# Output projection, norm and next products in one block by halves of the tokens

## The chip, the cores and the metric

The kernel runs on one core of a Trainium2 chip. The metric is the device time of one execution in microseconds, the median of several runs. TensorE does the matrix products into PSUM, VectorE (DVE) and ScalarE (ACT) work on SBUF and PSUM, GpSimd (POOL) on SBUF, and SyncE (SP) issues nearly all the DMAs.

## What is computed

The reference is two layers of a perceiver over 16 sequences of 64 tokens of 256 features, all float32. The part that matters here, cut:

```python
x = x + cross_attention(layernorm(x), ctx)         # 16 heads, 1601 keys
x = x + wide_attention(layernorm(x), context)      # 8 heads of 128, 1024 keys, Wout 1024 -> 256
x = x + merged_ffn(layernorm(x))                   # gates from relu(xn @ gate_w1 + b1), mean over tokens
x = x + shared_attention(layernorm(x), ctx)        # 16 heads of queries, one head of 1601 keys
x = x + alibi_attention(layernorm(x))              # 16 heads of 16, 64 keys, Wo 256 -> 256
h = layernorm(x)                                   # last layer: attention with rotary q and k,
x = x + moe(h)                                     # on rmsnorm(h) * ln1, then 8 experts, top 2
```

## The kernel before

`x` stays in SBUF as eight tiles of 128 tokens by 256 features (`TILES`), and is held by token. A product needs its input by feature, so each norm ends with 16 transposes on TensorE into four PSUM banks, which ScalarE moves into `xn_t` by halves of 512 tokens (`HALVES`). Everything is written in blocks: a block holds one instruction stream for each engine, ordered by hand with semaphores, and ends in a barrier of all engines.

Between an attention and the next products there are two blocks.

`add_projection` (a `dense_block`) does the output projection. TensorE fills one unit for each tile of tokens: 2 chunks of features for shared and alibi attention, 8 for the wide one, and a float32 product is two matmul instructions in the trace. VectorE adds the unit to `x` (L342), takes the statistics (L345) and aggregates them into `moments` (L346). Four units of two banks go round.

`norm_block` does the rest. SP issues the loads of this block and of what follows. VectorE adds epsilon to all eight variances at once (L163), ScalarE takes the root (L222), VectorE refines and inverts it in five small steps (L150 to L154), each waiting for the one before, and writes the eight normalized tiles (L177). The MoE norm does this twice, the second time into `again` (L170 to L187). TensorE transposes tile by tile (L200), ScalarE moves each half (L227), and then the tasks run in two units of two banks: TensorE multiplies (L215) and VectorE or ScalarE moves the result out (L320, L321, L326, L1923, L2180 to L2182). The tasks are

- FFN: two tasks of `gate_w1`, each over both halves, moved by VectorE and by ScalarE in turn;
- alibi: two tasks each of `wk` and `wq`, then four value tasks; GpSimd multiplies the attention's bias (L2143) when the loads are in;
- MoE: four rotary tasks of `wk`, four of `wq` (each with the swapped weights as well), all moved by VectorE in three operations, then four value tasks moved by ScalarE.

After the key tasks SP issues the copies of the keys into `k_blocks`, eight DMAs, and the block waits for them before it ends.

The norm ahead of shared attention has no tasks. It fills rows 64 and up of the three key and three query buffers with zeros, six memsets of GpSimd (L133). In `shared_attention_block` GpSimd then sets row 64 of the key buffers to one, the ones and zeros of `v`, the zeros of `k_blocks`, and adds the output bias to `x`. TensorE makes the four query units, SP stores and reloads them, and the ring of scores for the maxima (L1718, VectorE's L1812) starts when the first are back.

Of the kernel before, what the change touches and what calls it, by code (L numbers as in the profile page):

```python
# [12 lines left out]
F32 = mybir.dt.float32  # L13
I32 = mybir.dt.int32
ALU = mybir.AluOpType
# [3 lines left out]
P = 128  # L19
# [4 lines left out]
BANK = 512  # L24
# [213 lines left out]

def dense_block(core, name, tasks, copies=(), pool_program=None):
# [60 lines left out]


def feature_products(weights, m, src_t, chunks=CHUNKS, rows=P, cols=P):

    return [(lambda u, h=h: u[0:cols, h, :], weights[:, k, m * cols:(m + 1) * cols],
             src_t[:, k, h * BANK:(h + 1) * BANK], k == 0, k == chunks - 1, h)
            for h in range(HALVES) for k in range(chunks)]


def feature_tasks(core, jobs):

    nc = core.nc
    tasks = []
    for weights, m_tiles, src_t, dst, bias, relu in jobs:
        for m in range(m_tiles):
            def move_dve(unit, step, m=m, dst=dst, bias=bias, relu=relu):
                out = dst[:, m, :].rearrange("p (h n) -> p h n", h=HALVES)
                if bias is None:
                    return nc.vector.tensor_copy(out, unit)
                if relu:
                    return nc.vector.tensor_scalar(out, unit, bias[:, m:m + 1], 0.0, ALU.add, ALU.max)  # L320
                return nc.vector.tensor_scalar(out, unit, bias[:, m:m + 1], None, ALU.add)  # L321

            def move_act(unit, step, m=m, dst=dst, bias=bias, relu=relu):
                out = dst[:, m, :].rearrange("p (h n) -> p h n", h=HALVES)
                func = ACT.Relu if relu else (ACT.Copy if bias is None else ACT.Identity)
                return nc.scalar.activation(out, unit, func, bias=0.0 if bias is None else bias[:, m:m + 1])  # L326

            on = ("dve", "act")[len(tasks) % 2]
            tasks.append((feature_products(weights, m, src_t), move_dve if on == "dve" else move_act, on))
    return tasks  # L330
# [688 lines left out]
def wide_attention(core):  # L1019
# [5 lines left out]
    with ExitStack() as outer:  # L1025
# [14 lines left out]
        add_projection(core, "wide_out", heads_t, WIDE_HEADS, wout, x)  # L1040
# [232 lines left out]
def merged_ffn(core):  # L1273

    nc, dram, x = core.nc, core.dram, core.x
    with ExitStack() as outer:
        def sb(stack, name, shape):
            return core.sbuf(stack, f"ffn_{name}", shape)  # L1280

        xn_t, gate_t = (sb(outer, n, [P, CHUNKS, TOKENS]) for n in ("xn_t", "gate_t"))
        gate_tiles = {n: sb(outer, n, shape) for n, shape in (
            ("gw2", [P, CHUNKS, TASKS]), ("gw2_wide", [P, CHUNKS, P]), ("gb2_column", [TASKS, 1]), ("gb2_wide", [P, 1]),
            ("spread_mask", [P, SPREAD]), ("task_b1", [GATE_ROWS, HIDDEN]), ("task_b2", [GATE_ROWS, DIM]))}
        with ExitStack() as inner:
            gw1, gb1 = sb(inner, "gw1", [P, CHUNKS, DIM]), sb(inner, "gb1", [P, CHUNKS])
            xn = sb(inner, "xn", [P, TILES, DIM])
            norm_block(core, "ffn_norm", x, xn, xn_t, True, loads=[(gw1[:], dram["gate_w1"]), (gb1[:], dram["gate_b1"])] + [
                (t[:], dram[n]) for t, n in ((gate_tiles["gw2"], "gate_w2"), (gate_tiles["gw2_wide"], "gate_w2_wide"),  # L1290
                                             (gate_tiles["gb2_wide"], "gate_b2_wide"), (gate_tiles["spread_mask"], "spread_mask"),
                                             (gate_tiles["task_b1"], "ffn_task_b1"), (gate_tiles["task_b2"], "ffn_task_b2"))]
                + [(gate_tiles["gb2_column"][:], dram["gate_b2"].unsqueeze(1))],
                tasks=feature_tasks(core, [(gw1, CHUNKS, xn_t, gate_t, gb1, True)]), task_loads=2, moments_ready=True)
        merged_ffn_block(core, xn_t, gate_t, gate_tiles)


def merged_ffn_block(core, xn_t, gate_t, gate_tiles):

# [233 lines left out]
def shared_attention(core):  # L1533
# [3 lines left out]
    with ExitStack() as outer:  # L1537
        def sb(stack, name, shape, dtype=F32):
            return core.sbuf(stack, f"shared_{name}", shape, dtype)

        wo, heads_t = sb(outer, "wo", [P, CHUNKS, DIM]), sb(outer, "heads_t", [P, CHUNKS, TOKENS])
# [7 lines left out]
                   fills=[(t[SPLIT_ROWS:].bitcast(F32), 0.0) for t in (*k, *q)],  # L1549
# [4 lines left out]
        add_projection(core, "shared_out", heads_t, CHUNKS, wo, x)  # L1554


def shared_attention_block(core, k, q, wq, bq, v, v1, bv, bo, scratch, heads_t):
# [17 lines left out]
    with ExitStack() as stack:  # L1575
# [28 lines left out]
        queries_stored = sem("queries_stored")  # L1604
        ones_set = sem("ones_set")
# [30 lines left out]
        with core.block() as block:  # L1636
# [275 lines left out]
def value_tasks(nc, xn_t, wv, v):  # L1912
# [4 lines left out]
    for b0 in range(0, BATCH, per_unit):  # L1917
# [8 lines left out]
        tasks.append((products, move, "act"))  # L1926
    return tasks


# [919 lines left out]
```

## Time and profile before

| what | value |
|---|---|
| runs | 2371.7, 2373.8, 2376.3 us; median 2373.8 |
| profiled execution | 2377.7 us, span 2375.9 us |
| TensorE busy | 2179.1 us, 92% of the span |
| mean granted clock of TensorE | 0.952 |

The profile is one execution. A timeline row is a run of like instructions: its start in the span, its length from first start to last end, engine, line of the kernel, operation, result and operands, count, and in brackets how long the engine was idle before it and what it waited for. L50 in a bracket is the barrier between two blocks.

### The profile page before, as it was taken

How to read it: one execution, taken by the hardware profiler on the slowest of the kernel's cores; microseconds unless marked ns; L12 is line 12 of the kernel's file. 1: busy time of each engine (PE TensorE's matmuls, PEld its weight loads, DVE VectorE, ACT ScalarE, POOL GpSimd, SP SyncE). 2: the span in 40 equal slices, each digit the busy share in tenths (PEclk: the TensorE clock that was granted, in tenths of full speed). 3: DMA queues.
4: the chain of work that ended last, by engine and by line, in shares of the span. 5: the costliest groups of instructions: out<-in, count | busy, mean ns of one | idle time of the engine just before them, and what ended most of it. 6: DMA issues, size and time to landing. Idle time of an engine off the chain costs nothing. (4 is left out here: it accounts for less than half of the span.)

```text
span 2375.9 us, 39783 instructions
## 1 busy us (share of the span) xinstructions
PE 2179.1 (92%) x15922; PEld 1507.1 (63%) x15922; DVE 1314.4 (55%) x2266; ACT 994.0 (42%) x1858; POOL 332.1 (14%) x366
## 2 busy tenths in 40 slices
PE   7999999999999977999998799978999998877796
PEld 4777777777777754555564677844555554545695
DVE  4556556656665634555553344347777772656554
ACT  1555555555555551343332011114666663515121
POOL 3322222222222200000000000032000000000231
PEclk9999999999999978999999899988999999898798
DMA  6877776777777521000000221123112111023312
GB/s 202 197 167 182 178 168 150 171 176 167 183 179 169 127 58 50 6 12 6 6 1 1 114 86 74 54 48 74 32 28 35 31 17 39 2 55 133 134 48 78
DMA packets 100570, 216.18 MB, mean 91 GB/s; under 512 B 58482, under 2 KB 66043, under 8 KB 94660
## 3 DMA queue, kind: packets, MB, share of 16 engines
q1 hardware_dynamic: 97652, 204.93, 34.9%
q0 software_dynamic: 2208, 6.03, 0.8%
q10 hardware_dynamic: 528, 2.69, 0.4%
q8 instruction: 127, 2.08, 0.4%
q14 instruction: 55, 0.45, 0.1%
HBM read 91.16 MB, written 15.20 MB: 45 GB/s over the span
## 5 line engine op out<-in xcount | busy, mean ns | idle before, releaser
L908 DVE TENSOR_REDUCE L_xattn_maxima<-L_xattn_scores 128x1 f32<-128x1024 f32 (+1 forms) x256 | 253.5, 990 | 249.2 <-PE L_xattn_scores L831 248.8
L975 ACT ACTIVATE L_xattn_probs_t<-L_xattn_turned 128x1024 f32<-128x1024 f32 (+1 forms) x256 | 220.8, 862 | 342.3 <-PE L_xattn_turned L843 342.3
L1812 DVE TENSOR_REDUCE shared_half_maxima<-shared_ring 128x1 f32<-128x578 f32 (+1 forms) x251 | 244.3, 990 | 88.3 <-PE shared_ring L1718 85.2
L1892 ACT ACTIVATE shared_exps<-shared_scores 128x512 f32<-128x512 f32 (+1 forms) x416 | 225.7, 594 | 122.5 <-PE shared_scores L1739 121.8
L987 ACT ACTIVATE L_xattn_probs<-L_xattn_scores,L_xattn_maxima 128x1024 f32<-128x1024 f32 (+1 forms) x256 | 235.6, 925 | 37.9 <-DVE L_xattn_maxima L911 37.9
L843 PEld LDWEIGHTS L_xattn_turned<-ident,L_xattn_probs 128*128 128x128 f32 x1664 | 198.0, 144 | 81.0 <-issue 48.1
L843 PE MATMUL L_xattn_turned<-ident,L_xattn_probs 128*128 128x128 f32 x1664 | 234.7, 281 | 14.1 <-ACT L_xattn_probs_t L975 12.0
L505 PE MATMUL L_xattn_projected<-L_xattn_wv,L_xattn_ctx 128*128 128x256 f32 x780 | 193.6, 390 | 0.0
L499 PE MATMUL L_xattn_projected<-L_xattn_ctx,L_xattn_wk 128*128 128x400 f32 x480 | 181.9, 501 | 0.0
L831 PE MATMUL L_xattn_scores<-L_xattn_k_stack,L_xattn_q_stack 128*128 128x512 f32 (+1 forms) x512 | 159.5, 393 | 22.2 <-ACT L_xattn_probs L987 11.1
L1739 PE MATMUL shared_scores<-shared_q,shared_k 128*128 128x512 f32 (+1 forms) x416 | 154.4, 449 | 0.1
L505 PEld LDWEIGHTS L_xattn_projected<-L_xattn_wv,L_xattn_ctx 128*128 128x128 f32 x780 | 137.3, 187 | 21.6 <-issue 0.5
L1718 PE MATMUL shared_ring<-shared_k,shared_q 128*128 128x512 f32 x502 | 135.5, 368 | 10.7 <-DMA shared_q<-q_scratch 5.9
L468 POOL CAST L_xattn_k_part<-L_xattn_k_part 128x400 fp32r<-128x400 f32 (+1 forms) x128 | 66.4, 519 | 559.5 <-DVE L_xattn_k_part L529 559.5
L1251 ACT ACTIVATE wide_probs<-wide_scores,wide_stats 128x1024 f32<-128x1024 f32 x64 | 71.4, 1115 | 153.8 <-DVE wide_stats L1201 153.8
L470 POOL TENSOR_TENSOR L_xattn_k_part<-L_xattn_k_part 128x400 fp32r<-128x400 f32 (+1 forms) x128 | 132.8, 1037 | 10.3
L1380 PE MATMUL ffn_merging<-ffn_spread,ffn_task 128*128 128x256 f32 x512 | 129.8, 404 | 4.2 <-DVE ffn_merged L1459 4.2
L1753 PE MATMUL shared_weighed<-shared_exps,shared_v 128*32 128x256 f32 (+1 forms) x1664 | 132.9, 391 | 0.2 <-ACT shared_exps L1892 0.2
L499 PEld LDWEIGHTS L_xattn_projected<-L_xattn_ctx,L_xattn_wk 128*128 128x128 f32 x480 | 91.3, 190 | 46.4 <-issue 0.7
L1134 PE MATMUL wide_scores<-wide_k_t,wide_q_t 128*128 128x512 f32 x256 | 120.5, 593 | 0.0
L1156 PE MATMUL wide_weighed<-wide_probs_t,wide_v 128*128 128x512 f32 x256 | 115.6, 605 | 3.0 <-ACT wide_probs_t L1242 2.2
L1380 PEld LDWEIGHTS ffn_merging<-ffn_spread,ffn_task 128*128 128x128 f32 x512 | 93.1, 197 | 37.9 <-DVE ffn_merged L1459 12.4
(390 smaller groups left out, 3163.3 us busy)
## 6 DMA issues: line engine op xcount, KB each, us to landing
L_xattn_k_stack<-L_xattn_k_part SPq DMA_DIRECT2D x504, 200.2 KB, 4.3
L_xattn_ctx<-in_ctx_t SPq DMA_DIRECT2D x16, 1602.0 KB, 6.9
ffn_task<-in_ffn_task SPq DMA_DIRECT2D x16, 1024.0 KB, 6.7
experts_w_in<-in_expert_in SPq DMA_DIRECT2D x8, 1024.0 KB, 12.0
shared_k<-k_scratch SPq DMA_DIRECT2D x64, 100.1 KB, 3.3
L_xattn_q_stack<-q_scratch SPq DMA_DIRECT2D x128, 32.0 KB, 2.0
k_scratch<-L_xattn_shared_part SPq DMA_DIRECT2D x128, 32.0 KB, 1.7
shared_q<-q_scratch SPq DMA_DIRECT2D x64, 64.0 KB, 3.6
```

The costliest lines, as they stand in the source:

```text
L499: last = nc.tensor.matmul(bank[:, 0:w], wk[:, k, g * P:(g + 1) * P], ctx[parity][:, k, s:s + w], start=k == 0, stop=k == CHUNKS - 1)
L505: last = nc.tensor.matmul(bank[0:rows, i * DIM:(i + 1) * DIM], ctx[parity][:, k, t * P:t * P + rows], wv[:, k, :], start=k == 0, stop=k == ...
L831: last = nc.tensor.matmul(scores[:, s // BANK, 0:w], q_stack[parity][:, n].rearrange("p h q -> p (h q)"), k_stack[:, n, s:s + w], start=Tr ...
L843: last = nc.tensor.transpose(turned_tiles[:, i, :], probs[n % 2][:, t * P:(t + 1) * P], core.ident[:])
L908: nc.vector.reduce_max(maxima[n % 2][:, half:half + 1], cols, axis=AX).then_inc(halves_maxed, 1)
L975: nc.scalar.activation(probs_t[:, t:t + m, p * P:(p + 1) * P], turned_tiles[:, 0:m, :], ACT.Copy).then_inc(turned_moved, 1)
L987: nc.scalar.activation(probs[n % 2][:, lo:hi], scores_flat[:, lo:hi], ACT.Exp, bias=maxima[n % 2][:, 2:3], scale=SCALE, accum_out=sums[n / ...
L1380: last = nc.tensor.matmul(merging[:, n % 2, i * 2 * P:(i + 1) * 2 * P], block_of, spread[:].rearrange("p b f -> p (b f)"), start=True, sto ...
L1718: last = nc.tensor.matmul(banks[:, s // BANK - 2 * half, 0:w], q[slot][:, 2 * n:2 * n + 2, :].rearrange("r h q -> r (h q)"), k[slot][:, s: ...
L1739: nc.tensor.matmul(scores[0:m, h, :], k[slot][:, t * P:t * P + m], q[slot][:, h * 8:(h + 1) * 8, :].rearrange("r h q -> r (h q)"), start=T ...
L1812: nc.vector.reduce_max(half_maxima[:, n, half:half + 1], found[:, 0:HALF_STARTS[half + 1] - HALF_STARTS[half]], axis=AX).then_inc(ring_max ...
L1892: nc.scalar.activation(exps[n % 2][0:m, h * BANK:(h + 1) * BANK], scores[0:m, h, :], ACT.Exp, scale=SCALE).then_inc(exps_done, 1)
```

## The change

A new `joint_block` replaces `add_projection` and `norm_block` at three places: wide attention to FFN, shared to alibi attention, alibi to MoE attention. Inside it the four PSUM banks of `psum` serve the projection's tiles first and the tasks afterwards (four units of one bank; two of two banks for MoE), and four more take the transposes. VectorE adds and takes statistics for tiles 0 to 3, normalizes them, and then does the same for tiles 4 to 7. TensorE projects all eight tiles, transposes half 0, runs the first `turn_after` tasks, transposes half 1 and runs the rest. Tasks are now by halves: first all those that need half 0 (keys, queries, values), then those of half 1. ScalarE moves out the tasks of half 0, except the rotary ones.

```python
def joint_block(core, name, heads_t, chunks, weights, dst, dst_t, feature_scale=None, again=None, loads=(), task_loads=0, fills=(),
                tasks=(), unit_banks=1, turn_after=2, copies=(), keys_copied=None, copies_after=(), pool_program=None):
...
                # sync: loads, then
                for half, (half_copies, n) in enumerate(zip(copies, copies_after)):
                    for on in ("dve", "act"):
                        if moved_count(on, n):
                            sp.wait_ge(moved[on], moved_count(on, n))
                    for tile, view in half_copies:
                        sp.dma_start(tile, view).then_inc(keys_copied[half], 16)
...
                # tensor
                def run_task(i):
                    products, _, _, half = tasks[i]
                    if i < slots:
                        pe.wait_ge(row_added, per_half + unit_banks * (i + 1))
                    else:
                        on = tasks[i - slots][2]
                        pe.wait_ge(moved[on], moved_count(on, i - slots + 1))
                    pe.wait_ge(turned_moved, half + 1)
                    for part, lhs_t, rhs, start, stop in products:
                        last = nc.tensor.matmul(part(unit(i)), lhs_t, rhs, start=start, stop=stop)
                    last.then_inc(products_ready, 1)

                for t in range(TILES):
                    if t >= 4:
                        pe.wait_ge(row_added, t - 3)
                    for k in range(chunks):
                        last = nc.tensor.matmul(psum[:, t % 4, 0:DIM], heads_t[:, k, t * P:(t + 1) * P], weights[:, k, :],
                                                start=k == 0, stop=k == chunks - 1)
                    last.then_inc(row_done, 1)
                turn(0)
                pe.wait_ge(tasks_loaded, 16 * task_loads)
                for i in range(turn_after):
                    run_task(i)
                turn(1)
                for i in range(turn_after, len(tasks)):
                    run_task(i)
...
                # vector
                for half in range(HALVES):
                    rows = range(half * per_half, (half + 1) * per_half)
                    variance = moments[:, half * per_half:(half + 1) * per_half, 1]
                    for t in rows:
                        dve.wait_ge(row_done, t + 1)
                        nc.vector.tensor_tensor(x[:, t, :], psum[:, t % 4, 0:DIM], x[:, t, :], ALU.add).then_inc(row_added, 1)
                        dve.wait_ge(row_added, t + 1)
                        step(nc.vector.bn_stats(stats[:, t, :], x[:, t, :]))
                        nc.vector.bn_aggr(moments[:, t, :], stats[:, t, :]).then_inc(own_step, 1)
                        steps[0] += 1
                    dve.wait_ge(own_step, steps[0])
                    step(nc.vector.tensor_scalar(spread[0][half][:, 0], variance, LN_EPS, None, ALU.add))
                    inverse_root(0, half)
                    for t in rows:
                        ins = nc.vector.tensor_scalar(dst[:, t, :], x[:, t, :], moments[:, t, 0:1],
                                                      rstd[0][half][:, t % per_half:t % per_half + 1], ALU.subtract, ALU.mult)
...
                    if again is not None:
...
                        inverse_root(1, half)
                        for t in rows:
                            nc.vector.tensor_scalar(again[:, t, :], dst[:, t, :], rstd[1][half][:, t % per_half:t % per_half + 1],
                                                    None, ALU.mult).then_inc(rows_ready, 1)
                dve.wait_ge(tasks_loaded, 16 * task_loads)
                for i, (_, move, on, _) in enumerate(tasks):
                    if on == "dve":
                        dve.wait_ge(products_ready, i + 1)
                        move(unit(i), step).then_inc(moved["dve"], 1)
...
                # scalar
                for i in range(rounds):
                    root(i, 0)
                move_turned(0)
                for i in range(rounds):
                    root(i, 1)
                act.wait_ge(tasks_loaded, 16 * task_loads)
                run_moves(0, turn_after)
                move_turned(1)
                run_moves(turn_after, len(tasks))
```

(The four comments that name an engine stand for the lines that open its stream.) The callers:

```diff
-        add_projection(core, "wide_out", heads_t, WIDE_HEADS, wout, x)
+            joint_block(core, "ffn_joint", heads_t, WIDE_HEADS, wout, xn, xn_t_next,
...
+                        + [(gate_tiles["gb2_column"][:], dram["gate_b2"].unsqueeze(1))], task_loads=2, turn_after=CHUNKS,
+                        tasks=[task for half in range(HALVES) for task in half_tasks(
+                            core, gw1, xn_t_next, gate_t, gb1, True, half, ("act",) if half == 0 else ("act", "dve"))])
...
-        norm_block(core, "alibi_norm", x, xn, xn_t, True, fills=[(v[:, :, :, HEAD_DIM:HEAD_DIM + 1], 1.0)],
...
+        for half in range(HALVES):
+            tasks += half_tasks(core, wk, xn_t, k_t, bk, False, half, ("act",))
+            tasks += half_tasks(core, wq, xn_t, q_t, bq, False, half, ("act",) if half == 0 else ("dve",))
+            tasks += [task for task in value_tasks(nc, xn_t, wv, v) if task[3] == half]
+        per_half = len(tasks) // HALVES
+        joint_block(core, "alibi_joint", heads_t, CHUNKS, core.shared_wo, xn, xn_t, fills=[(v[:, :, :, HEAD_DIM:HEAD_DIM + 1], 1.0)],
...
+                    task_loads=5, tasks=tasks, turn_after=4, copies=key_block_copies(core, k_t), keys_copied=keys_copied,
+                    copies_after=(CHUNKS, per_half + CHUNKS), pool_program=make_bias)
...
+        tasks = [task for half in range(HALVES) for task in products if task[3] == half]
+        per_half = len(tasks) // HALVES
+        joint_block(core, "moe_joint", core.heads_t, CHUNKS, core.alibi_wo, h, hn_t, core.ln1, again=hn,
...
+                    task_loads=7, tasks=tasks, unit_banks=2, turn_after=2, copies=key_block_copies(core, k_t), keys_copied=keys_copied,
+                    copies_after=(CHUNKS, per_half + CHUNKS))
```

The keys are copied into `k_blocks` by halves, sixteen DMAs, and each score of the attention waits for its half (`keys_copied`), not the block. `heads_t` and the two output weights move to an outer scope, as they now live across the blocks. Shared attention's fills leave its norm:

```diff
-                   fills=[(t[SPLIT_ROWS:].bitcast(F32), 0.0) for t in (*k, *q)],
...
                 for i in range(BUFFERS):
+                    if i == 1:
+                        pool.wait_ge(low_ready, len(query_units))
+                    for tile in (q[i], k[i]):
+                        nc.gpsimd.memset(tile[SPLIT_ROWS:].bitcast(F32), 0.0).then_inc(zeros_set, 1)
+                    pool.wait_ge(zeros_set, 2 * (i + 1))
                     nc.gpsimd.memset(k[i][SPLIT_ROWS:SPLIT_ROWS + 1, :].bitcast(F32), 1.0).then_inc(ones_set, 1)
```

## Rows read from the trace of the kernel before

**Rows 1.** The page, busy time, share of the span and instructions.

```profile
PE 2179.1 (92%) x15922; PEld 1507.1 (63%) x15922; DVE 1314.4 (55%) x2266; ACT 994.0 (42%) x1858; POOL 332.1 (14%) x366
```

**Rows 2.** Stretches: start:end, length, TensorE busy (count), granted clock, DMA share, GB/s.

```profile
1590.30:1595.20 4.90, 4.90 (x6) 0.50 0.85 143
1599.90:1605.70 5.80, 0.00 (x0) 0.69 0.59 135
1605.80:1608.90 3.10, 3.10 (x8) 0.50 1.11 368
...
2001.60:2015.60 14.00, 14.00 (x35) 1.00 0.30 54
2059.60:2076.40 16.80, 12.57 (x156) 0.50 0.01 2
...
2094.30:2121.80 27.50, 27.50 (x64) 1.00 0.23 38
```

**Rows 3.** Timeline around the shared norm: start, length, engine, line, operation [idle before].

```profile
1578.92 4.20 POOL L133 MEMSET shared_k<- 64x1602 f32 x3 [648.74 <-POOLq L50]
...
1580.93 0.82 DVE L153 TENSOR_SCALAR shared_norm_spread<-shared_norm_spread 128x8 f32<-128x8 f32 x1
...
1582.02 5.65 DVE L177 TENSOR_SCALAR moe_hn<-x,moments,shared_norm_rstd 128x256 f32<-128x256 f32 x8
1583.07 3.17 POOL L133 MEMSET shared_q<- 64x1024 f32 x3
...
1605.76 1.22 PE L1718 MATMUL shared_ring<-shared_k,shared_q 128*128 128x512 f32 x2 [5.90 <-DMA shared_q<-q_scratch]
...
1607.02 1.23 DVE L1812 TENSOR_REDUCE shared_half_maxima<-shared_ring 128x1 f32<-128x1024 f32 x1 [5.65 <-PE shared_ring L1718]
```

**Rows 4.** Timeline from the wide projection to the FFN block.

```profile
1300.18 27.86 PE L277 MATMUL wide_out_psum<-wide_wout,wide_heads_t 128*128 128x256 f32 x128 [1.05 <-PEq L50]
...
1329.47 1.28 ACT L222 ACT_TABLE_LOAD   x1 [40.37 <-PEq L50]
...
1331.64 0.17 DVE L153 TENSOR_SCALAR ffn_norm_spread<-ffn_norm_spread 128x8 f32<-128x8 f32 x1
...
1332.09 2.68 DVE L177 TENSOR_SCALAR ffn_xn<-x,moments,ffn_norm_rstd 128x256 f32<-128x256 f32 x8
...
1335.96 7.03 PE L215 MATMUL ffn_norm_psum<-ffn_xn_t,ffn_gw 128*128 128x512 f32 x16
1336.16 1.08 ACT L227 ACTIVATE ffn_xn_t<-ffn_norm_turned 128x512 f32<-128x512 f32 x2 [0.51 <-PE ffn_norm_turned L200]
...
1344.54 0.07 DVE L1478 MEMSET ffn_gates<- 9x16 f32 x1 [3.58 <-PEq L50]
```

**Rows 5.** Timeline of TensorE inside alibi's attention.

```profile
2039.82 1.09 PE L2012 MATMUL alibi_turned<-ident,alibi_probs 128*128 128x128 f32 x8
```

**Rows 6.** Timeline from the shared projection to alibi's attention.

```profile
1990.99 0.18 DVE L346 BATCH_NORM_AGGREGATE moments<-stats 128x2 f32<-128x6 f32 x1
...
1994.94 0.18 DVE L346 BATCH_NORM_AGGREGATE moments<-stats 128x2 f32<-128x6 f32 x1
...
2003.23 1.90 POOL L2143 TENSOR_TENSOR alibi_bias<-alibi_distance,alibi_slopes 128x1024 f32<-128x1024 f32 x1 [7.36 <-DMA alibi_bo<-in_L_attn_bo]
...
2010.14 5.50 SPq L122 DMA_DIRECT2D k_blocks<-alibi_k_t  x8
...
2015.62 7.21 PE L215 MATMUL alibi_norm_psum<-alibi_wv,alibi_xn_t 128*64 128x128 f32 x128
...
2023.75 1.28 ACT L2105 ACT_TABLE_LOAD   x1 [0.27 <-PEq L50]
```

**Rows 7.** Timeline from the alibi projection to the MoE attention.

```profile
2079.04 0.18 DVE L346 BATCH_NORM_AGGREGATE moments<-stats 128x2 f32<-128x6 f32 x1
...
2122.01 0.69 DVE L2180 TENSOR_TENSOR moe_q_part_cos<-moe_norm_psum,moe_cos 128x512 f32<-128x512 f32 x1 [1.42 <-PE moe_norm_psum L215]
...
2130.45 1.28 ACT L2105 ACT_TABLE_LOAD   x1 [0.27 <-PEq L50]
```

More of the change, by code:

```diff
@@ new lines, in half_products, with half_tasks, move_dve, move_act @@
+def half_products(weights, m, src_t, half, chunks=CHUNKS):
+    return [(lambda u: u[:, 0, :], weights[:, k, m * P:(m + 1) * P], src_t[:, k, half * BANK:(half + 1) * BANK],
+             k == 0, k == chunks - 1) for k in range(chunks)]
+def half_tasks(core, weights, src_t, dst, bias, relu, half, engines):
+    nc = core.nc
+    tasks = []
+    for m in range(CHUNKS):
+        def move_dve(unit, step, m=m):
+            out = dst[:, m, half * BANK:(half + 1) * BANK]
+            if relu:
+                return nc.vector.tensor_scalar(out, unit[:, 0, :], bias[:, m:m + 1], 0.0, ALU.add, ALU.max)
+            return nc.vector.tensor_scalar(out, unit[:, 0, :], bias[:, m:m + 1], None, ALU.add)
+        def move_act(unit, step, m=m):
+            return nc.scalar.activation(dst[:, m, half * BANK:(half + 1) * BANK], unit[:, 0, :], ACT.Relu if relu else ACT.Identity,
+                                        bias=bias[:, m:m + 1])
+        on = engines[m % len(engines)]
+        tasks.append((half_products(weights, m, src_t, half), move_dve if on == "dve" else move_act, on, half))
+    return tasks
@@ L299, in _ @@
                         move(psum[:, 2 * (i % units):2 * (i % units) + 2, :], None).then_inc(moved["act"], 1)
[L302 to L330, printed above, removed]
 def add_projection(core, name, heads_t, chunks, weights, x, limit=None):
@@ L1924, in move, with self_attention_block @@
                                         unit[:, 0, :].rearrange("p (n d) -> p n d", d=HEAD_DIM), ACT.Copy)
-        tasks.append((products, move, "act"))
+        tasks.append((products, move, "act", b0 * HALVES // BATCH))
     return tasks
 def key_block_copies(core, k_t):
-    return [(core.k_blocks[j * HEAD_DIM:(j + 1) * HEAD_DIM, :, j, :], k_t[j * HEAD_DIM:(j + 1) * HEAD_DIM, :, :])
-            for j in range(GROUP_HEADS)]
-def self_attention_block(core, name, q_t, v, bias, bv, heads_t, fills=(), out_bias=None):
+    return [[(core.k_blocks[j * HEAD_DIM:(j + 1) * HEAD_DIM, :, j, half * BANK:(half + 1) * BANK],
+              k_t[j * HEAD_DIM:(j + 1) * HEAD_DIM, :, half * BANK:(half + 1) * BANK]) for j in range(GROUP_HEADS)]
+            for half in range(HALVES)]
+def self_attention_block(core, name, q_t, v, bias, bv, heads_t, keys_copied, out_bias=None):
     nc = core.nc
+    core.counted += [copied.num for copied in keys_copied]
     SCALE = float(HEAD_DIM) ** -0.5
@@ L1981, in _ @@
             def _(sp):
[L1982 to L1985 removed]
+                for copied in keys_copied:
+                    sp.wait_ge(copied, 16 * GROUP_HEADS)
             @block.gpsimd
@@ L2184, in move @@
                 return last
-            tasks.append((products, move, "dve"))
+            tasks.append((products, move, "dve", h))
     return tasks
```

216 lines of the change are left out of this document (160 added, 56 removed).

## The prediction

> **What bounds the kernel now.** I read the page first: TensorE is busy 2179 of 2376 us [rows 1], so an edit that rearranges VectorE or ScalarE work pays only where TensorE stands idle. The diff touches three places where an attention's output projection is followed by a layer norm and the next products, and one norm alone (shared attention's). These are four stretches of 15 to 60 us, so I read the timeline of each, instruction by instruction. The reader is to see two things. Each joint today is a chain: the projection, then VectorE's norm with TensorE idle, then TensorE's products, a last move out of PSUM and a block barrier. And in alibi and MoE the products are long, so the end is TensorE's: once its transposes have begun it hardly waits. There only an earlier start of that stream, or a hole put into it, counts. The table of stretches shows TensorE's granted clock, 0.50 (1.2 GHz) after some holes and 1.00 (2.4 GHz) in full streams [rows 2].
>
> **Shared norm without its fills.** Today GpSimd's six memsets start with the block and last until 1586.2. Beside them the eight row passes of VectorE take 5.65 us; the same eight take 2.68 where GpSimd is quiet. One 8-column step takes 0.82 where its like takes 0.17 [rows 3, 4]. All of it is ahead of the transposes and the queries: 2.97 + 0.65 = 3.6 us gone. The fills move into the attention block. Slot 0 (zeros 1.06 + 1.4, ones another 1.4) is ready some 4 us into the block, while the ring's first product comes 15 us into it, after a DMA [rows 3]: the queries hide it. GpSimd then waits for the last query; behind that wait stand slots 1 and 2 (8 us in all), which batch 1's ring needs only after the 16 units of batch 0, and the ones of `v`, the memset of `k_blocks` and the bias addition, all about 11 us later than today, beside the maxima of batches 0 and 1. Those read PSUM, and one took 1.23 us while GpSimd was filling [rows 3], no more than elsewhere. Only the small combination of maxima (SBUF to SBUF) can meet a memset: 0 to 0.65 us, I take 0.3. The queries run at half clock for their first 4.9 us [rows 2]; with the transposes earlier and denser that can vanish (2.5 us gained) or stay; I take that it stays. Gain 3.3, bounds 2 and 6.
>
> The Trainium skill (SBUF — State Buffer, "SBUF: two separate sides") says that a GpSimd operation and a VectorE operation in a 2-port mode exclude each other for a whole instruction. The trace shows row passes of 0.7 us beside memsets of 1.4, which is a slowing and no exclusion; by the rule, the bias product in the alibi joint would cost 1.9 us where I take 1.3, and the sum would be 0.6 smaller.
>
> **FFN joint.** The projection is TensorE's, 27.9 us for eight tiles, 3.45 each [rows 4]. VectorE needs 1 us a tile (below, in alibi), so the norm of tiles 0 to 3 (1.6 us of small steps and root, 1.3 of rows) fits between later tiles, and TensorE isn't delayed. The activation table load, 1.28 us on the path, was released by the barrier, not by its input [rows 4]; in the joint it runs at the block's start, under the projection. After the projection's end (1328.05): eight transposes 1.1 to 1.3 us (1.09 at full clock [rows 5]), two moves 1.1, ready at 1330.5. Two half products, 4 instructions of 0.43 each (16 took 7.03 [rows 4]), to 1333.95. VectorE's second norm: last tile done 1329.2, but its square root stands behind the moves of the first half in ScalarE's queue, so 1330.7, then 1.05 of steps and 1.34 of rows, 1333.15: in time. Transposes to 1335.15, moves to 1336.3, two products to 1339.8, VectorE's half move 0.7, barrier 0.3: 1340.85, where today the next block starts at 1344.54 [rows 4]. Gain 3.7, bounds 3 and 4.3.
>
> **Alibi joint.** Here the projection is VectorE's. Tile 3 is done at 1991.17 and tile 7 at 1995.12, 0.99 a tile [rows 6]. Half 0's norm: spread and root 0.55, steps 1.05, rows 1.34, to 1994.15; TensorE ends its tiles at 1991.4 and waits. Transposes end at 1994.45, moves at 1995.6. From there TensorE has 4 half products 6.9, transposes 1.2, two value tasks 3.5 (128 instructions took 7.21 for four) and 0.4 for the switch to 64 columns, 4 half products with a switch 7.1, two values 4.0: 23.1 us; then the move 0.65 and the barrier 0.28. Next block at 2019.6 against 2023.75 [rows 6]: 4.1 us by this. VectorE's second half is ready at 2001.1, before TensorE wants it at 2002.5. Two costs come off. GpSimd's bias product, 1.90 us, starts 7.8 us after the block's first load, when the loads are in [rows 6]; the same distance from 1984.35 puts it at 1992.2 to 1994.1, on the steps and rows of half 0. At the rate of the shared norm (3.6 us lost beside 7.4 of memsets) it costs 0.9, at most 1.9. I take 1.3. The other is the clock. Between 1991.4 and 1997 TensorE does only eight transposes. After 5.8 us idle (1599.9 to 1605.7) the products came at 0.50, and products at 0.50 lasted 3.1 and 4.9 us [rows 2]. Today's hole in alibi is hidden, since the slow clock falls on the transposes and the products come at 1.00 [rows 2]. In the joint the products themselves follow the hole: half of 4 us, 2.0 lost (bounds 0 and 2.5). Gain 4.1 - 1.3 - 2.0 = 0.8, bounds -0.5 and 3.5.
>
> The Trainium skill (TensorE: Matmul & The Clock Gate, "Why this matters for your kernels") advises against idle gaps between bursts of matmuls, since the clock falls back to half. That speaks against this edit in the alibi joint, and the trace agrees; with the rule set aside the sum would be 2 us larger.
>
> **MoE joint.** Tile 3 is done at 2079.22 [rows 7]. Half 0: first norm 1.6 + rows 1.34, three steps 0.6, root and way 0.35, five steps 1.05, second rows 1.1: 6.1 us, to 2085.3. Transposes end 2086.2, moves 2087.65, and products start, where today they start at 2094.3 [rows 2]. But VectorE, which must also move every rotary product (three operations of 0.69, 2.0 us [rows 7]), first does tiles 4 to 7 (3.95) and the second norm (6.1), to 2095.35. TensorE has two units only: it runs the two key tasks (3.44 each) and the transposes, and stands until task 0 is moved at 2097.4. This hole swallows most of the clock's 2 us: full clock 2097.45, half 2097.8. From there: two query tasks 6.9, two values 4.0, four tasks 13.95, two values 4.0, move and barrier 0.9: 29.75. Next block at 2127.55 against 2130.45 [rows 7]: gain 2.9, bounds 1.5 and 3.3; I take 2.8.
>
> **Costed at nothing.** Sixteen key copies of half size instead of eight: SP issued eight in 5.5 us [rows 6]. Those of half 0 go out under products; those of half 1 (alibi from 2012.5, MoE from 2118) end before the blocks do, and are wanted first by unit 4 of 8. If that cover were gone: up to 5.5 us each. SP has only its waits queued behind them. The wait of each score on its copies is met. The joints' weight loads go out during the projection, earlier than needed.
>
> **Sum.** 3.3 + 3.7 + 0.8 + 2.8 = 10.6 us. Against the profiled execution, 2377.7 (span 2375.9), that gives 2367.1. The median of the runs, 2373.8, lies 3.9 below it: 2363.
>
> **Rivals.** (a) The holes are harmless: the clock stays at 1.00 in alibi (2), the bias product meets little (1), and the queries after the shared norm find full clock (2.5): 16 us, 2358. For it: not every hole was followed by a slow stretch; against: eight transposes in 5 us are little work. Chance 0.15. (b) The joints give little beyond the fills: alibi -0.5, MoE 1.5, shared norm 2.5, FFN 3, so 6.5, and with one more fall of the clock in an attention behind, 4: 2369.5. Chance 0.17. (c) The halves don't take effect: ScalarE reloads its table between root and copies, or the second half's root behind the first half's moves holds VectorE; only the 3.6 of the fills stays, 2370. Against: in today's norm one load serves root, copies and moves [rows 4]. Chance 0.06. (d) Slower: once fallen in the alibi and MoE holes, the clock stays at 0.50 through the products. It stood at 0.50 for 17 us in the attention before MoE [rows 2]. From 10.6 us lost beyond what I count, 5.3 per joint (10.6 of products each at half clock), the gain is gone; with alibi's 14 us of half products and as much in MoE it is 14 lost: 2377. Against: full streams came back within 5 us. Chance 0.05. The forecast: 0.57. What a measurement of this kernel can tell from no change begins at about 0.2%, 4.7 us, so faster means under 2369.1. The forecast and (a) hold 0.72, (b) half of its 0.17: 0.80 faster; same 0.15, slower 0.05. The range, 2356 to 2370.5, leaves out (d) and the tail of (a) beyond its sum.
>
> **What would show it.** Shared row passes at 0.33 us each, and the first query product 3.6 us sooner behind the FFN. In the FFN joint a table load at the block's start and 12.8 us from the projection's last matmul to the next block (16.5 today). In alibi, slower row passes beside the bias product, then key products at 0.86 us each. In MoE, TensorE waiting for VectorE's first rotary move. I am wrong if the row passes of half 0 don't start until the last tile, or if products run at 0.50 for over 5 us.

## The result, and the profile after

The changed kernel takes 2358.9 us (median of 4 runs, 2351.3 to 2361.6) against 2375.0 (4 runs, 2371.7 to 2376.3): ratio 0.9936, 95% interval 0.9919 to 0.9952. A second set gave 2356.4 (6 runs) against 2369.2 (17, of which one at 3175.8, with a low clock throughout, is left out of the ratio), 0.9942 [0.9921, 0.9962]. So the change gives 12.7 to 16 us; forecast were 10.6, to 2363. The profiled execution took 2351.3, its span 2349.1.

On the page TensorE's busy time falls from 2179 [rows 1]:

```profile
PE 2168.8 (92%) x15922; PEld 1499.2 (64%) x15922; DVE 1315.5 (56%) x2292; ACT 997.3 (42%) x1868; POOL 331.6 (14%) x366
```

It executes the same 15922 matmuls. But the two profiles also differ by 9.6 us in the first attention, which no edit touches: from the start to its output projection it took 901.0 before and 891.4 after, and 891.0 to 899.4 in the twelve experiments. The whole profile can't be used as the measure, so I compare stretches, each from one tile's last or first record (weight loads count) to the next block's first (microseconds; "again" is a second profile of the same changed kernel):

| stretch | before | after | again | what changed |
|---|---|---|---|---|
| last wide head to the FFN block | 45.3 | 41.7 | 41.7 | -3.6 |
| FFN down to the first shared query | 13.4 | 9.9 | 9.9 | -3.5 |
| first query to the first exponent | 40.2 | 39.1 | 39.3 | -1.0 |
| last shared rows to alibi's scores | 40.4 | 37.2 | 37.3 | -3.2 |
| alibi's last rows to MoE's scores | 59.9 | 57.5 | 56.8 | -2.4, -3.1 |

**The shared norm**, timeline (start, length, engine, line, operation [idle before]), against [rows 3]:

```profile
1567.86 0.17 DVE L153 TENSOR_SCALAR shared_norm_spread<-shared_norm_spread 128x8 f32<-128x8 f32 x1
...
1568.31 2.68 DVE L177 TENSOR_SCALAR moe_hn<-x,moments,shared_norm_rstd 128x256 f32<-128x256 f32 x8
...
1573.82 0.95 POOL L1875 MEMSET shared_q<- 64x1024 f32 x1 [652.74 <-POOLq L50]
...
1588.27 1.22 PE L1903 MATMUL shared_ring<-shared_k,shared_q 128*128 128x512 f32 x2 [7.44 <-DMA shared_q<-q_scratch]
...
1589.53 1.23 DVE L1997 TENSOR_REDUCE shared_half_maxima<-shared_ring 128x1 f32<-128x1024 f32 x1 [7.19 <-PE shared_ring L1903]
...
1593.03 13.77 POOL L1881 MEMSET k_blocks<- 128x16384 f32 x1
```

The row passes are back at 2.68 for eight and the small step at 0.17: both lost times are gone. The first memset now starts with the queries, and the ring's first product still waits for its queries' DMA, 14.5 us into the block. The maximum beside the memsets takes 1.23, as before.

**The FFN joint**, timeline, against [rows 4]:

```profile
1290.55 1.28 ACT L396 ACT_TABLE_LOAD   x1 [11.01 <-PEq L50]
1290.59 27.86 PE L327 MATMUL ffn_joint_psum<-wide_wout,wide_heads_t 128*128 128x256 f32 x128 [1.05 <-PEq L50]
...
1318.29 1.04 PE L307 MATMUL ffn_joint_turned<-ident,ffn_xn 128*128 128x128 f32 x8
...
1319.36 1.08 ACT L402 ACTIVATE ffn_xn_t<-ffn_joint_turned 128x512 f32<-128x512 f32 x2 [13.08 <-PE ffn_joint_turned L307]
...
1320.33 0.21 ACT L396 ACTIVATE ffn_joint_spread<-ffn_joint_spread 128x4 f32<-128x4 f32 x1
...
1320.59 3.67 PE L320 MATMUL ffn_joint_psum<-ffn_xn_t,ffn_gw 128*128 128x512 f32 x8 [1.27 <-ACT ffn_xn_t L402]
...
1326.40 3.67 PE L320 MATMUL ffn_joint_psum<-ffn_xn_t,ffn_gw 128*128 128x512 f32 x8 [1.27 <-ACT ffn_xn_t L402]
...
1331.28 0.07 DVE L1659 MEMSET ffn_gates<- 9x16 f32 x1 [0.34 <-PEq L50]
```

The table load runs under the projection, which isn't longer than it was; the transposes of half 0 follow its last matmul at once. From the projection's start to the next block it is 40.69 us; the forecast chain has 1340.85 - 1300.18 = 40.67.

**The alibi joint**, timeline, against [rows 6]:

```profile
1967.10 8.83 PE L327 MATMUL alibi_joint_psum<-shared_wo,heads_t 128*128 128x256 f32 x32 [0.71 <-PEq L50]
...
1975.31 2.96 DVE L371 TENSOR_SCALAR alibi_xn<-x,moments,alibi_joint_rstd 128x256 f32<-128x256 f32 x4
...
1975.77 1.08 PE L307 MATMUL alibi_joint_turned<-ident,alibi_xn 128*128 128x128 f32 x6
1976.20 1.92 POOL L2331 TENSOR_TENSOR alibi_bias<-alibi_distance,alibi_slopes 128x1024 f32<-128x1024 f32 x1 [8.54 <-DMA alibi_bo<-in_L_attn_bo]
...
1978.32 0.44 PE L307 MATMUL alibi_joint_turned<-ident,alibi_xn 128*128 128x128 f32 x2 [1.47 <-DVE alibi_xn L371]
...
1980.03 3.67 PE L320 MATMUL alibi_joint_psum<-alibi_xn_t,alibi_wk 128*128 128x512 f32 x8 [1.27 <-ACT alibi_xn_t L402]
...
2003.27 1.28 ACT L2290 ACT_TABLE_LOAD   x1 [0.27 <-PEq L50]
```

The bias product meets the rows, as forecast: 2.96 us for four where they take 1.38 alone. But the eight key products take 3.67, full clock. The table of stretches shows it too: 0.51 inside the projection and 1.00 in the key products (columns as in [rows 2]; the stretch between them, with the transposes, was at 1.00 too):

```profile
1967.90:1971.30 3.40, 3.40 (x10) 0.51 0.55 158
...
1978.80:1992.00 13.20, 11.97 (x89) 1.00 0.23 40
2063.60:2070.30 6.70, 5.25 (x12) 0.50 0.00 0
```

**The MoE joint**, timeline, against [rows 7] (the last stretch above is its clock):

```profile
2063.59 1.97 PE L307 MATMUL moe_joint_turned<-ident,moe_hn 128*128 128x128 f32 x8 [2.86 <-DVE moe_hn L384]
...
2067.00 3.62 PE L320 MATMUL moe_joint_psum<-moe_hn_t,moe_wk 128*128 128x512 f32 x4 [1.45 <-ACT moe_hn_t L402]
...
2074.11 0.69 DVE L2373 TENSOR_TENSOR moe_k_part_cos<-moe_joint_psum,moe_cos 128x512 f32<-128x512 f32 x1
...
2076.48 1.88 PE L320 MATMUL moe_joint_psum<-moe_hn_t,moe_wq 128*128 128x512 f32 x4
...
2106.79 1.28 ACT L2290 ACT_TABLE_LOAD   x1 [0.56 <-PEq L50]
```

TensorE waits 2.86 us for VectorE's second norm, then turns and multiplies at half clock. The slow 3.62 us cost almost nothing at the end: the query products want the first rotary move, which VectorE ends at 2076.1, and they start at 2076.48. From tile 3 (2058.41) to the next block are 48.4 us; the forecast has 2127.55 - 2079.22 = 48.3.

### The profile page after: what moved, and what is told of

It reads as the page before. It is cut to its first block and busy times, and to the rows that moved or that the text cites. A ratio compares the mean times of both kernels' runs of the same rounds, so it can differ in the third digit from the quotient of the medians.

```text
span 2349.1 us, 39843 instructions
## 1 busy us (share of the span) xinstructions
PE 2168.8 (92%) x15922; PEld 1499.2 (64%) x15922; DVE 1315.5 (56%) x2292; ACT 997.3 (42%) x1868; POOL 331.6 (14%) x366
## 5 line engine op out<-in xcount | busy, mean ns | idle before, releaser
L1024 PEld LDWEIGHTS L_xattn_turned<-ident,L_xattn_probs 128*128 128x128 f32 x1664 | 197.3, 144 | 79.7 <-issue 46.7
L651 POOL TENSOR_TENSOR L_xattn_k_part<-L_xattn_k_part 128x400 fp32r<-128x400 f32 (+1 forms) x128 | 132.8, 1037 | 10.3
```

Source lines behind the costliest of these rows:

```text
L1024: last = nc.tensor.transpose(turned_tiles[:, i, :], probs[n % 2][:, t * P:(t + 1) * P], core.ident[:])
```

## Experiments

**One part each.** Four kernels have one part of the change and the rest as in the kernel before; a fifth has the new functions and none of the parts. All five are written in the changed kernel's file, with the parts that they leave out put back to the calls, tasks and key copies of before. For the FFN joint, cut:

```diff
-            joint_block(core, "ffn_joint", heads_t, WIDE_HEADS, wout, xn, xn_t_next,
...
+            add_projection(core, "wide_out", heads_t, WIDE_HEADS, wout, x)
...
+                tasks=feature_tasks(core, [(gw1, CHUNKS, xn_t_next, gate_t, gb1, True)]), task_loads=2, moments_ready=True)
```

> Only the shared zeros are moved; all three joints are as before. As forecast: row passes of 2.7 us instead of 5.65 and 3.3 us less than before. Rival, the queries also find full clock since the transposes are earlier and denser: 4.6 to 6 less, first query products 0.43 us apart. Rival, the later memsets take it back: under 2.

> Only the FFN joint; zeros, alibi and MoE as before. As forecast: 3.7 us less than before, 13.2 us from the last projection start to the next block. Rival, the gain of the changed kernel comes from elsewhere: this is within 1 us of before.

> Only the alibi joint. As forecast (clock falls in TensorE's hole, products at 0.86 us each for some 4 us): 0.8 us less than before. Rival (the slow clock already in the projection makes TensorE end its tiles as the first rows come, so there is no long hole and no fall): 3.2 us less, products at 0.43.

> Only the MoE joint. As forecast: 2.8 us less than before, a hole of 3 us in TensorE, clock 0.50 in the first products, and TensorE's third task waiting for or just meeting VectorE's first move. Rival, the joint also speeds the attention behind by the instant at which the clock changes: 5 us less. If all four of these sum to some 16 us they add; if they sum to 11, the rest is in their interplay.

> All parts undone in the changed kernel's own file: the blocks of before, with the buffers of the changed kernel (the same work as before, other places in SBUF, and the projection weights held in the outer scope). If placement or run to run drift makes part of the 14 us: over 2 us from before. Theory: within 1 us of before.

| kernel | this, before (us) | ratio, 95% | its own stretch | 
|---|---|---|---|
| fills moved | 2367.95, 2369.44 | 0.9988 [0.9975, 1.0000] | 13.4 to 10.0, exponent 38.9 after the query |
| FFN joint | 2366.14, 2369.44 | 0.9976 [0.9965, 0.9988] | 45.2 or 46.7 to 41.7 |
| alibi joint | 2367.44, 2369.44 | 0.9985 [0.9975, 0.9994] | 40.4 to 38.8 |
| MoE joint | 2367.78, 2369.44 | 0.9990 [0.9980, 0.9999] | 59.9 to 58.1 |
| none | 2369.64, 2369.44 | 1.0003 [0.9992, 1.0013] | all as before |

By the ratios the first four make 0.61% together, 14.5 us, each known to some 0.1%; all parts in one kernel gave 0.64% and 0.58%. By the medians of the table the four make only 8.5 us, so the whole times can't say whether the parts add. The interval of the fills reaches 1.0000. The stretches are sharper: 3.4 + 3.5 + 1.6 + 1.8 = 10.3 us, against 12.7 to 13.4 in the changed kernel. The fills and the FFN joint give alone what they give together; the alibi and the MoE joint gave less, and the clock is where they differ (below). Without all parts nothing is left.

The FFN joint was worth most. Its old form stands at 45.2 or 45.3 in the profiles of before, of the MoE joint alone and of "none", and at 46.7 in those of the fills and of alibi alone. The difference lies in the old products. Fills alone, timeline:

```profile
1325.96 3.67 PE L200 MATMUL ffn_norm_turned<-ident,ffn_xn 128*128 128x128 f32 x16 [4.51 <-DVE ffn_xn L177]
1329.43 8.28 PE L215 MATMUL ffn_norm_psum<-ffn_xn_t,ffn_gw 128*128 128x512 f32 x16
```

After the same idle 4.5 us, the 16 products took 8.28 and in the kernel before 7.03 [rows 4]. Most of it comes back: the FFN block behind took 231.3 us in both profiles with 46.7, and 232.3 in the three with 45.2 or 45.3. The joint has no such hole, and stood at 41.7 in each of its eight profiles with halves.

With the alibi joint alone the joint gives 1.6, not 3.2. Its timeline, and the table of stretches:

```profile
1984.32 2.96 DVE L371 TENSOR_SCALAR alibi_xn<-x,moments,alibi_joint_rstd 128x256 f32<-128x256 f32 x4
```

```profile
1984.79 1.08 PE L307 MATMUL alibi_joint_turned<-ident,alibi_xn 128*128 128x128 f32 x6
1987.34 0.44 PE L307 MATMUL alibi_joint_turned<-ident,alibi_xn 128*128 128x128 f32 x2 [1.47 <-DVE alibi_xn L371]
1989.04 5.37 PE L320 MATMUL alibi_joint_psum<-alibi_xn_t,alibi_wk 128*128 128x512 f32 x8 [1.27 <-ACT alibi_xn_t L402]
```

```profile
1984.80:1989.40 4.60, 1.86 (x10) 1.00 0.00 0
1989.40:1992.80 3.40, 3.40 (x5) 0.50 0.00 0
```

Same order, same waits of 1.47 and 1.27 us, and here the clock falls at 1989.4, in the middle of the key products: 5.37 instead of 3.67. So the fall that I had taken as certain exists, costs 1.7, and comes or doesn't.

The MoE joint alone gives 1.8, not 2.4 or 3.1. Timeline:

```profile
2078.19 3.75 PE L320 MATMUL moe_joint_psum<-moe_hn_t,moe_wk 128*128 128x512 f32 x4 [1.45 <-ACT moe_hn_t L402]
2081.73 3.08 PE L320 MATMUL moe_joint_psum<-moe_hn_t,moe_wk_swapped 128*128 128x512 f32 x4
```

The second group of key products is slow too, 3.08 for 1.88. TensorE then never waits for a rotary move, and from tile 3 to the next block are 49.4 us, where the changed kernel takes 48.2 to 48.4: a slow stretch 1.2 us longer is no longer hidden.

**The changed kernel again, the bias later, and a bridge for MoE's hole.** The first is the changed kernel. In the second GpSimd waits for the last row before the bias product:

```diff
                 if pool_program is not None:
                     pool.wait_ge(loaded, 16 * (len(loads) - task_loads))
+                    pool.wait_ge(rows_ready, TILES)
                     pool_program(pool)
```

In the third TensorE gets 20 transposes of the identity, into a bank that is overwritten, ahead of MoE's first real ones:

```diff
+                if again is not None:
+                    for i in range(20):
+                        nc.tensor.transpose(turned[:, HALVES * (i % CHUNKS) + 1, 0:P], core.ident[:], core.ident[:])
                 turn(0)
```

> The changed kernel as it is, for its time beside the next three and for a second trace. If the four parts of the first experiments add, some 14 us less than before. In the alibi joint either the clock holds (products 0.43 us each, as in its first trace) or it falls during the products (as in the kernel with the alibi joint alone): theory of the instant. If it holds again in alibi and the joint gives 3.2 us again, the order of work decides and not the instant.

> The changed kernel, with GpSimd's bias product of alibi held back until all eight rows are normalized. Theory (it slows VectorE's rows of half 0, 2.96 us for four instead of 1.34): rows 1.34 us, transposes and products 1.6 us earlier, 1.6 less than the changed kernel. Rival (what the rows gain is lost since the clock then falls or the bias is late for the attention): no change.

> The changed kernel with 20 transposes of the identity, into PSUM that is written again later and read by nobody before, put into TensorE's hole in the MoE joint. Extra work, same result. Theory (the hole makes the clock fall, and the products after it run at half speed for 3 to 6 us): clock 1.00 in the first products, the next block 0.3 us earlier where VectorE's late moves hide the loss, and 1.6 to 2 where they don't. Rival (the clock falls all the same, or the filling delays the transposes): no change or slower by under 1.

The changed kernel again: 12.7 us less than before by the medians, 0.58% or 13.7 us by the ratio, so the 14 expected lies within the interval. In alibi the clock held again and the joint gave 3.1. The kernel with the fall has another kernel's stages ahead of it, so whether its order of work or the chance of an execution decides stays open.

Bias later: 2352.3 us, 0.9926 [0.9906, 0.9946], against 0.9942 [0.9921, 0.9962] for the changed kernel on the same chip. The medians are 4.1 apart, the intervals overlap; the profile is clear. Rows of half 0, bias product:

```profile
1977.06 1.38 DVE L372 TENSOR_SCALAR alibi_xn<-x,moments,alibi_joint_rstd 128x256 f32<-128x256 f32 x4
```

```profile
1985.50 1.90 POOL L2332 TENSOR_TENSOR alibi_bias<-alibi_distance,alibi_slopes 128x1024 f32<-128x1024 f32 x1 [16.21 <-DVE alibi_xn L372]
```

The rows take 1.38, and from tile 3 to the next block are 27.95 us where the changed kernel takes 29.52 (29.55 in its second profile): 1.57 less, which is the 2.96 - 1.38 of the rows. The contention costs what the rows show, one for one.

How it acts is seen on single instructions. Of the four row passes in the changed kernel, the median is 408 ns and the longest 1989:

```profile
L371 DVE TENSOR_SCALAR alibi_xn<-x,moments,alibi_joint_rstd x4: 406/408/1989, 1975.3 to 1976.3; 128x256 f32<-128x256 f32 x4
```

The last pass starts at 1976.3, a tenth behind the 1.92 us product, and lasts until the product is over; the other three are untouched. It waited for the whole product: 1989 - 408 is the 1.58 lost. In the kernel before, the row passes beside the `shared_q` memsets read the same way once they are looked at one by one:

```profile
1583.07 2.13 POOL L133 MEMSET shared_q<- 64x1024 f32 x2
...
1583.19 2.15 DVE L177 TENSOR_SCALAR moe_hn<-x,moments,shared_norm_rstd 128x256 f32<-128x256 f32 x2
```

Two passes to two memsets, in step. The 0.7 us a pass of the prediction was the mean over four passes beside memsets, of over 1 us each, and four that ran after the last one at 0.33.

With the bridge: 2357.2 us, 0.9943 [0.9924, 0.9962], no change. The real transposes came at full clock, and it still fell behind them, by the wait for ScalarE's moves:

```profile
2068.02 2.35 PE L332 MATMUL moe_joint_turned<-ident 128*128 128x128 f32 x20
2071.17 1.23 PE L307 MATMUL moe_joint_turned<-ident,moe_hn 128*128 128x128 f32 x8 [0.80 <-DVE moe_hn L387]
2073.84 3.59 PE L320 MATMUL moe_joint_psum<-moe_hn_t,moe_wk 128*128 128x512 f32 x4 [1.45 <-ACT moe_hn_t L405]
```

But the second profile of the changed kernel, without a bridge, has nearly the same two numbers, 1.23 and 3.52. So this run shows that one bridge isn't enough, and not that it did anything:

```profile
2066.59 1.23 PE L307 MATMUL moe_joint_turned<-ident,moe_hn 128*128 128x128 f32 x8 [2.98 <-DVE moe_hn L384]
...
2069.27 3.52 PE L320 MATMUL moe_joint_psum<-moe_hn_t,moe_wk 128*128 128x512 f32 x4 [1.45 <-ACT moe_hn_t L402]
```

**Without the halves.** One block per joint, but VectorE takes in all eight tiles before it norms either half:

```diff
+                def take(rows):
                     for t in rows:
...
+                if name in ('ffn_joint', 'alibi_joint', 'moe_joint'):
+                    take(range(TILES))
+                for half in range(HALVES):
```

> The changed kernel with the joints still one block each, but VectorE takes all eight tiles before it normalizes either half. If the halves are what pays: FFN gives 0.8 instead of 3.7, alibi 0.4 instead of 3.2, MoE 0.7 instead of 2.8, in all 7 to 8 us slower than the changed kernel. Rival (the merged block, the hidden table load and the missing barriers pay): under 3 us slower.

Measured 2374.1 us against 2369.2: 1.0021 [1.0005, 1.0036], so 17.7 more than the changed kernel on the same chip, and slower than the kernel before. The 7 to 8 us expected were too few: I had each joint keep a little gain, and each lost. The FFN stretch takes 48.1 (41.7 with halves, 45.3 before), alibi 42.4 (37.2, 40.4), MoE 60.8 (57.5, 59.9). FFN, timeline:

```profile
1322.18 1.62 PE L307 MATMUL ffn_joint_turned<-ident,ffn_xn 128*128 128x128 f32 x8 [3.17 <-DVE ffn_xn L377]
...
1324.81 0.21 ACT L402 ACTIVATE ffn_joint_spread<-ffn_joint_spread 128x4 f32<-128x4 f32 x1
...
1325.07 6.16 PE L320 MATMUL ffn_joint_psum<-ffn_xn_t,ffn_gw 128*128 128x512 f32 x8 [1.27 <-ACT ffn_xn_t L408]
...
1333.36 3.67 PE L320 MATMUL ffn_joint_psum<-ffn_xn_t,ffn_gw 128*128 128x512 f32 x8 [1.27 <-ACT ffn_xn_t L408]
```

The norm is again after the projection, the first products behind its hole are slow (6.16 for 3.67), and the products wait 1.27 for ScalarE's moves twice. In this form one block instead of two is worth nothing by itself, and all of the joints' gain is the half that is ready early. This kernel still has its tasks by halves, with the two waits; one block with whole tasks wasn't tried.

**Both of MoE's holes bridged; rows straight from x.** The bridge with nine more idle transposes behind `turn(0)`; then a kernel in which MoE's normed rows come straight from `x` with the product of both factors, the once-normed rows are written later, one behind each rotary move, and the bias is late; then both.

```diff
+                        step(nc.vector.tensor_tensor(rstd[1][half][:], rstd[1][half][:], rstd[0][half][:], ALU.mult))
...
-                            nc.vector.tensor_scalar(again[:, t, :], dst[:, t, :], rstd[1][half][:, t % per_half:t % per_half + 1],
-                                                    None, ALU.mult).then_inc(rows_ready, 1)
+                            normalise(t, again, rstd[1][half]).then_inc(rows_ready, 1)
```

> The changed kernel with 20 transposes of the identity after the MoE projection and 9 more after the transposes of half 0, so that both holes of TensorE ahead of the first products are filled. Extra work, same result. Theory (the clock falls by the holes): clock 1.00 in all products of the MoE joint, its end 0 to 0.5 us sooner since VectorE's first move comes at the same time. Rival (what runs in the holes doesn't hold the clock): it falls again; time as the changed kernel.

> The changed kernel with the late bias product, and with MoE's second normalized rows taken straight from x (both factors multiplied first); the rows of h itself are written between VectorE's later moves. Theory (VectorE's chain of 6.1 us for each half starts the MoE products and holds their first move): rows of half 0 some 1.5 us sooner, first rotary move 3 us sooner, next block 1.5 us sooner; with the 1.5 of the bias 3 us less than the changed kernel. Rival (the later moves become late instead): 1.5 us less only.

> Both of the above together. Now that VectorE's first move is 3 us sooner, the clock of the first products is no longer hidden: with the clock held at 1.00 the next block comes 1.5 us sooner than without the fillings; if the clock isn't held, no difference.

Ratios are to the kernel before on the same chip (2369.4 for the last three). The last column is free of the projection's clock.

| kernel | median | ratio, 95% | MoE stretch | tile 3 to the next block |
|---|---|---|---|---|
| changed, first and second profile | 2358.9, 2356.4 | 0.9936, 0.9942 | 57.5, 56.8 | 48.4, 48.2 |
| both holes bridged | 2356.0 | 0.9942 [0.9929, 0.9955] | 56.5 | 48.2 |
| rows straight from x | 2352.1 | 0.9926 [0.9913, 0.9938] | 54.2 | 46.3 |
| both | 2353.2 | 0.9933 [0.9921, 0.9945] | 54.1 | 46.2 |

Both holes bridged, timeline and table of stretches:

```profile
2066.90 1.96 PE L320 MATMUL moe_joint_psum<-moe_hn_t,moe_wk 128*128 128x512 f32 x4 [0.47 <-ACT moe_hn_t L408]
...
2076.82 1.55 PE L320 MATMUL moe_joint_psum<-moe_hn_t,moe_wq 128*128 128x512 f32 x3 [1.49 <-DVE moe_k_t L2381]
```

```profile
2060.00:2087.00 27.00, 23.92 (x133) 1.00 0.16 32
```

Now the clock stays at 1.00, the key products take 1.96 instead of 3.62, and TensorE gives 1.49 of it back waiting for VectorE's first rotary move. From tile 3 to the next block it takes 48.2, as the second profile of the changed kernel does. So there the half clock is hidden, and VectorE is the bound of that stretch; with the MoE joint alone, where it lasted longer, it wasn't. The kernel with rows straight from `x` takes work from VectorE's chain ahead of that move: 1.9 us less from tile 3 on where 1.5 were expected, and the same within 0.1 with the bridges. The 1.5 us more that I expected of the bridges there didn't come: with the clock held at 1.00, TensorE again waited, 1.09 us, for the first rotary move. In the whole time the 1.9 doesn't show: the ratio is 0.9926, as for the late bias alone. It is small beside the spread of the untouched stages.

## Why the prediction was right, point by point

- **Shared norm without its fills: right.** Forecast 3.6 less 0.3; measured 3.5 in the stretch, no lengthened combination of maxima. I took that the half clock in the queries stays, and that was wrong: they took 9.60 us before and 7.10 in the changed kernel, all at 1.00. These are the 2.5 of rival (a), but they don't reach the end, and the 1.0 behind the norm isn't theirs. With the fills alone the queries ran 9.01 us, partly at half clock, and the first exponent came 38.9 after the first query; in the changed kernel it came at 39.1. The ring waits for the DMA, and in the kernels that keep the old fills the stretch took 39.0 to 40.2. The combination of maxima took 0.17 throughout, also beside the 13.77 us memset; the 0.3 set aside for it wasn't needed.
- **FFN joint: right.** 3.7 forecast, 3.6 measured against the profile of before, and every instruction of the chain in its order, the second square root behind the moves included. (A tile of the projection is 3.48 us, not 3.45; nothing hangs on it.) What I left out is that the old form's products take 1.25 more in some executions, of which the block behind gives 1.0 back.
- **Alibi joint: the order right, the size wrong**, 0.8 against 3.2. The failing step is "TensorE ends its tiles at 1991.4 and waits", with the "half of 4 us, 2.0 lost" built on it. The trace of before has the end of the tiles:

```profile
1984.40 8.83 PE L277 MATMUL shared_out_psum<-shared_wo,shared_heads_t 128*128 128x256 f32 x32 [0.71 <-PEq L50]
```

  They end at 1993.2, not 1991.4, as the clock stands at half for part of them, and by then the first normed row is ready. The hole that I had there, from 1991.4 to some 1993.1, is gone; a pause of 1.47 behind the bias product and one of 1.27 for the moves are left. (By the prediction's own chain the products start at 1995.6, so the "1997" in its clock term was too late as well.) In four of five profiles with this order the clock didn't fall behind them; with alibi alone it did, and cost 1.7. So 2.0 was a fair price for a fall, taken as certain where it is the exception. The second term held: bias contention 1.6, taken 1.3. Without either cost the joint gives 32.58 - 27.95 = 4.6 from tile 3 on (bias late), where 4.1 was forecast.
  The Trainium skill (TensorE: Matmul & The Clock Gate, "Why this matters for your kernels") advises against idle gaps between bursts of matmuls, longer ones than these pauses. By the traces the clock fell behind even these in one profile of five, with 5.37 for 3.67.
- **The contention's kind: wrong.** "A slowing and no exclusion" came from a mean over eight. One pass of 1989 ns beside a product of 1916 is exclusion, as the Trainium skill (SBUF — State Buffer, "SBUF: two separate sides") has it. The size came out between my 1.3 and the 1.9 that I had worked out by the rule: 1.58, as the waiting pass would have needed its own 0.4 anyway.
- **MoE joint: right.** 2.8 forecast, 2.4 and 3.1 measured. From tile 3 on it is 48.4 against 48.3; the 0.5 between the profiles is ahead of tile 3, in the clock of the projection (7.7 us from its start after, 7.0 before and again). That the hole swallows the slow clock was shown by bridging it (48.2 with the clock held, 48.2 and 48.4 without). It swallows only so much: with the MoE joint alone the slow products lasted longer, and 49.4 were left.
- **Costed at nothing.** The 16 key copies were never waited for: TensorE's waits in both attentions of the profile after name ScalarE, VectorE and the block's start, and no DMA.
- **Sum.** 3.5 + 3.6 + 3.2 + 2.4 to 3.1 are 12.7 to 13.4 against 10.6. The profiled execution is 26.4 us shorter than that of before; 9.6 of that is the first attention and some 3 are in later stages that the change doesn't touch. Why the first attention varies wasn't tried.
- **Luck in the total.** The forecast, 2363, is 4 to 7 us above the medians measured, and rival (a)'s 2358 is nearer to both. Of (a)'s three terms only one came, the 2 us of alibi's clock; its bias product cost more than I took, not less, and its full clock in the queries gained nothing at the end. The forecast is right for the shared norm, FFN and MoE one by one; the total misses by what alibi has wrong and by what the spread of the stages adds.

## What to carry to other kernels

Merge a projection with the norm behind it only if the norm can start before the projection ends: the merger without the halves was slower than none, and the halves carried the gain. Look at single instructions beside a GpSimd operation before calling a contention a rate; and put GpSimd's work behind the last row pass that someone waits for. A slow clock behind a hole is worth a repair only where TensorE, and no other engine's move, is next in line, or where the slow stretch outlasts that move.

## What the runs showed of the hardware

- The same instructions with the same waits ran at either clock. The old FFN products took 7.03 or 8.28 behind 4.5 us idle, alibi's key products 3.67 or 5.37 behind pauses of 1.47 and 1.27.
- A VectorE row pass (`tensor_scalar`) of 0.41 us took 1.99 beside a GpSimd `tensor_tensor` of 1.92, and two row passes 2.15 beside two memsets of 2.13 together. Maxima out of PSUM kept their 1.23 beside memsets, and a small `tensor_tensor` in SBUF its 0.17.
- Idle transposes of 0.12 us each in both of TensorE's holes went with key products of 1.96 us in both profiles that have them; in the seven MoE joints without the second bridge these took 3.4 to 3.8. A bridge in the second hole alone wasn't tried.
- One untouched stage, the first attention, took 891 to 901 us from execution to execution, most of what the whole change is worth; the one behind it took 396 to 398 us, and 407 in one profile.
